# Order of the VectorE and GpSimd work in a merged LSTM and expert stage

## What is computed

```
# LSTM, 128 steps, one after the other (twice in this stage: layer 1 and layer 2)
z = x_t @ Wx + b + h @ Wh;  i, f, o, g = split(z)
c = sigmoid(f) * c + sigmoid(i) * tanh(g);  h = sigmoid(o) * tanh(c)

# expert block on the first LSTM's output, added to x
logits = a @ Wr + br;  the best two of 16 experts, with normalised softmax weights
h = layernorm(a @ W1[e] + b1[e]) * g1[e] + be1[e];  y = gelu(h) @ W2[e] + b2[e]
x = x + sum over the best two of weight * y
```

## Time and profile before

| | us |
|---|---|
| median of three runs | 4663.28 (4662.86 to 4663.63) |
| the profiled execution | 4662.41 |
| its span, first to last instruction | 4660.6 |
| the stage of the change | some 805, from about 1430 to 2235 |

### The profile page before, as it was taken

One profiled execution on the slowest core, in us unless ns is written; L12 is line 12 of the kernel. 1 busy time (PEld: TensorE's weight loads), 2 busy tenths in 40 slices (PEclk: granted clock), 3 DMA queues, 4 the chain that ended last, 5 costly groups with the idle time before them and its releaser, 6 DMA issues. The chain is left out here.

```text
span 4660.6 us, 118083 instructions
## 1 busy us (share of the span) xinstructions
PE 4309.6 (92%) x41087; PEld 3214.5 (69%) x41087; DVE 2494.8 (54%) x7506; ACT 1859.3 (40%) x4669; POOL 761.1 (16%) x3314
## 2 busy tenths in 40 slices
PE   6999999999998999998799999999997887889998
PEld 4556777777876888886355787787875555566666
DVE  5775664555554777776555444666666563421111
ACT  4433443333331444444233222666664452333333
POOL 1111220000001555554122000111111210000000
PEclk9999999999998999998699998999998997989999
DMA  1000000000000000000000000000000100000000
GB/s 53 0 0 25 0 0 25 0 0 0 0 0 10 1 2 1 1 1 1 33 1 0 3 0 0 3 3 3 3 3 2 52 0 1 0 1 0 0 0 18
DMA packets 3080, 28.73 MB, mean 6 GB/s; under 512 B 320, under 2 KB 832, under 8 KB 1216
## 3 DMA queue, kind: packets, MB, share of 16 engines
q1 hardware_dynamic: 2768, 24.81, 1.4%
HBM read 22.71 MB, written 2.10 MB: 5 GB/s over the span
## 5 line engine op out<-in xcount | busy, mean ns | idle before, releaser
L2231 DVE SCALAR_TENSOR_TENSOR experts_acc<-banks,experts_gate,experts_acc 128x128 f32<-128x128 f32 x512 | 144.2, 345 | 461.7 <-PE banks L2177 460.6
L2177 PEld LDWEIGHTS banks<-weights,experts_hidden 128*128 128x128 f32 x2560 | 303.3, 192 | 55.0 <-issue 49.7
L604 DVE TENSOR_REDUCE cells_row_max<-banks 128x4 f32<-128x512 f32 x384 | 238.5, 684 | 161.6 <-PE banks L397 161.6
L2177 PE MATMUL banks<-weights,experts_hidden 128*128 128x128 f32 x2560 | 305.2, 275 | 0.0
L761 PE MATMUL banks<-clock_fill 128*128 128x512 bf16 x932 | 284.8, 394 | 7.4 <-DVE wave_bias_parts L1612 7.4
L2450 ACT ACTIVATE experts_hidden<-banks,weights 128x512 f32<-128x512 f32 x256 | 175.8, 687 | 268.5 <-PE banks L2447 265.2
L1412 PEld LDWEIGHTS banks<-act_a,weights 128*128 128x128 f32 x2032 | 256.1, 196 | 25.6 <-DVE act_a L1670 18.0
L2447 PE MATMUL banks<-act_a,weights 128*128 (+1 forms) x512 | 262.3, 643 | 0.7 <-ACT experts_hidden L2450 0.3
L1412 PE MATMUL banks<-act_a,weights 128*128 (+1 forms) x2032 | 248.7, 281 | 10.8 <-DVE act_a L1670 10.7
L541 ACT ACTIVATE cells_probs<-banks 128x512 f32<-128x512 f32 x384 | 198.2, 603 | 95.0 <-PE banks L437 90.0
L604 DVE TENSOR_REDUCE attn_row_max<-banks 128x4 f32<-128x512 f32 x256 | 159.0, 684 | 134.8 <-PE banks L397 134.8
(11 more groups left out here) (522 smaller groups left out, 9904.5 us busy)
## 6 DMA issues: line engine op xcount, KB each, us to landing
weights<-in_p SPq DMA_DIRECT2D x1, 2894.5 KB, 17.2
weights<-in_p SPq DMA_DIRECT2D x1, 2894.0 KB, 9.2
weights<-in_p SPq DMA_DIRECT2D x2, 1364.0 KB, 7.1
x_res<-in_x SPq DMA_DIRECT2D x1, 2048.0 KB, 14.9
out_x<-x_res SPq DMA_DIRECT2D x1, 2048.0 KB, 6.3
weights<-in_p SPq DMA_DIRECT2D x1, 1836.0 KB, 10.9
weights<-in_p SPq DMA_DIRECT2D x1, 1835.5 KB, 6.9
weights<-in_p SPq DMA_DIRECT2D x1, 1344.5 KB, 9.8
```

Of the source, the lines that this page charges most:

```text
L604: dve.tensor_reduce(mt[:, 4 * g:4 * g + 4], bank, AX_X, ALU.max).then_inc(s["max_ready"], 1)
L2177: last = pe.matmul(ps[:, 2 + e % 2, t * P:(t + 1) * P], hs[lo:lo + n, (tile + f) % slots, t * P:(t + 1) * P], out_rhs(e, f, lo, n), start= ...
L2231: last = dve.scalar_tensor_tensor(out=acc[:, t, :], in0=ps[:, 2 + e % 2, t * P:(t + 1) * P], scalar=g[:, t, e:e + 1], in1=acc[:, t, :], op ...
```

## The change

Nothing is added to what is computed. On VectorE, `sums` and `guess` now stand ahead of `units`, and `add` comes last. The seventeen routing operations of a group are handed out one at a time: six places in the body (ahead of the cell, behind it, behind the state, between `sums` and `guess`, behind `units`, at the end). The semaphore `dist_ready` is gone: ScalarE's `distance` waits for the twelfth routing operation, which is the last of the second step, in the body's last place. On GpSimd, `tile_sum` stands ahead of `newton`, and the root has one operation less: the square is scaled by the root of 1/(2P), so that the sums are half the variance already, and the guess's constant is changed to fit (the third operation of a round is 1.5 - z in place of z + 1.5).

```diff
@@ GpSimd
             def newton(n, q):
                 pool.wait_ge(s["guess_ready"], n + 1)
                 past(pool, s["newton"], at)
-                pool.tensor_tensor(hv, v, newton_const[:, 0, :], ALU.mult).then_inc(s["newton"], 1)
                 for r in range(3):
                     pool.tensor_tensor(z, y, y, ALU.mult).then_inc(s["newton"], 1)
...
             def body(st, known):
+                it = item(st, SUM, known)
+                if it is not None and it[2] == 3:
+                    tile_sum(it[0], it[1], (st.c - SUM) // 4 % 2)
                 tile = tile_at(st, HSRC, known)
...
-                it = item(st, SUM, known)
-                if it is not None and it[2] == 3:
-                    tile_sum(it[0], it[1], (st.c - SUM) // 4 % 2)
@@ ScalarE
             def distance(group):
-                act.wait_ge(s["dist_ready"], group + 1)
+                act.wait_ge(s["route"], group * ROUTING + 12)
                 act.activation(dist[:, :], dist[:, :], ACT.Tanh, scale=0.5).then_inc(s["dist_tanh"], 1)
@@ VectorE
+            def route(st, known, at):
+                part_ = (st.c - ROUTE) % WAVE_PERIOD
+                group = group_at(st, part_, known) if part_ < 3 else None
+                if group is None or (part_, at) == (2, 5):
+                    return
+                done = group * ROUTING + (6 * part_ + at)
+                if part_ or at:
+                    dve.wait_ge(s["route"], done)
...
+                if part_ == 1:
+                    pick_best(at, work[:, :, :], m2, hot2, routed)
+                    if at == 5:
+                        past(dve, s["gates_ready"], group)
+                        routed(dve.tensor_tensor(dist[:, :], m1[:, :], m2[:, :], ALU.subtract))
...
             def body(st, known):
-                for part_, route in enumerate((route_first, route_second, route_gates)):
-                    group = group_at(st, part_, known)
-                    if group is not None:
-                        route(group)
+                route(st, known, 0)
                 cell(st, lo, hi)
+                route(st, known, 1)
                 tile = tile_at(st, LOGITS, known)
...
                 state(st, lo, hi)
+                route(st, known, 2)
+                it = item(st, HID, known)
+                if it is not None:
+                    sums(it[0], it[2])
+                    route(st, known, 3)
+                    guess(it[0], it[2])
+                else:
+                    route(st, known, 3)
+                it = item(st, UNIT, known)
+                if it is not None:
+                    units(it[0], it[2])
+                route(st, known, 4)
                 it = item(st, OUTPUT, known)
                 if it is not None:
                     add(st, *it)
-                it = item(st, UNIT, known)
-                if it is not None:
-                    units(it[0], it[2])
-                it = item(st, HID, known)
-                if it is not None:
-                    sums(it[0], it[2])
-                    guess(it[0], it[2])
+                route(st, known, 5)
```

More of the change, by code:

```diff
@@ L1226, in lstm_experts_lstm_stage @@
     RSRC, HSRC, GSRC = 4, 16, 20
-    NEWTON, ROUTING = 12, 15
+    NEWTON, ROUTING = 11, 16
     FOLD, FOLD_BIAS = (0, 2, 4, 5), 7
@@ L1255, in lstm_experts_lstm_stage @@
         sq = sb("square", [P, 2, 4, P + 1])
-        var, half_var, inv, part = (sb(n, [P, 2, 4]) for n in ("variance", "half_variance", "inverse", "part"))
+        half_var, inv, part = (sb(n, [P, 2, 4]) for n in ("half_variance", "inverse", "part"))
         shifted = sb("variance_shifted", [P, 2, 4], I32)
@@ L1546, in square @@
                 act.activation(sq[:, q % 2, :, 0:P], ps[:, HBANK + q % 2, :].rearrange("p (e j) -> p e j", e=4),
-                               ACT.Square, scale=float(P) ** -0.5).then_inc(s["square_ready"], 1)
+                               ACT.Square, scale=float(2 * P) ** -0.5).then_inc(s["square_ready"], 1)
             def gate_tanh(st, lo, hi):
@@ L1675, in logits @@
                                   ALU.add).then_inc(s["lg_ready"], 1)
-            def link(ins, group, n):
-                ins.then_inc(s["route"], 1)
-                dve.wait_ge(s["route"], group * ROUTING + n)
             over = lambda t: t[:, :].unsqueeze(2).broadcast_to([P, 4, NE])
             tie = const("tie16").unsqueeze(1).broadcast_to([P, 4, NE])
[L1685 to L1691, removed]
@@ L1693, in route_first @@
-            def route_first(group):
-                dve.wait_ge(s["lg_ready"], group * 4 + 4)
-                values = lg[:, tok(group * 4, 4), :]
[L1696 to L1713, removed]
+            def pick_best(at, values, top, hot, routed):
+                if at == 0:
+                    routed(dve.tensor_reduce(top[:, :], values, AX_X, ALU.max))
+                if at == 1:
+                    routed(dve.tensor_tensor(hot[:, :, :], values, over(top), ALU.is_equal))
+                if at == 2:
+                    routed(dve.tensor_tensor(hot[:, :, :], hot[:, :, :], tie, ALU.mult))
+                if at == 3:
+                    routed(dve.tensor_reduce(best[:, :], hot[:, :, :], AX_X, ALU.max))
+                if at == 4:
+                    routed(dve.tensor_tensor(hot[:, :, :], hot[:, :, :], over(best), ALU.is_equal))
@@ new lines, in route @@
+            def route(st, known, at):
[6 more added lines that the diff above has]
+                    dve.wait_ge(s["route"], done)
+                routed = lambda ins: ins.then_inc(s["route"], 1)
+                values = lg[:, tok(group * 4, 4), :]
+                if part_ == 0:
+                    if at == 0:
+                        dve.wait_ge(s["lg_ready"], group * 4 + 4)
+                    pick_best(at, values, m1, hot1, routed)
+                    if at == 5:
+                        routed(dve.scalar_tensor_tensor(out=work[:, :, :], in0=hot1[:, :, :], scalar=-1.0e30,
+                                                        in1=values, op0=ALU.mult, op1=ALU.add))
+                if part_ == 1:
+                    pick_best(at, work[:, :, :], m2, hot2, routed)
+                    if at == 5:
+                        past(dve, s["gates_ready"], group)
+                        routed(dve.tensor_tensor(dist[:, :], m1[:, :], m2[:, :], ALU.subtract))
+                if part_ == 2:
+                    if at == 0:
+                        routed(dve.tensor_tensor(work[:, :, :], hot1[:, :, :], hot2[:, :, :], ALU.subtract))
+                    if at == 1:
+                        routed(dve.tensor_tensor(hot1[:, :, :], hot1[:, :, :], hot2[:, :, :], ALU.add))
+                    if at == 2:
+                        dve.wait_ge(s["dist_tanh"], group + 1)
+                        routed(dve.tensor_tensor(work[:, :, :], work[:, :, :], over(dist), ALU.mult))
+                    if at == 3:
+                        routed(dve.tensor_tensor(hot1[:, :, :], hot1[:, :, :], work[:, :, :], ALU.add))
+                    if at == 4:
+                        dve.tensor_scalar(gates[:, tok(group * 4, 4), :], hot1[:, :, :], 0.5, None,
+                                          ALU.mult).then_inc(s["gates_ready"], 1)
@@ L1725, in guess @@
                 past(dve, s["unit_ready"], n - 1)
[L1726 to L1727 removed]
+                dve.tensor_scalar(inv[:, q % 2, :].bitcast(I32), shifted[:, q % 2, :], -1.0,
+                                  float(0x5F3759DF - 0x400000), ALU.mult, ALU.add).then_inc(s["guess_ready"], 1)
             def units(n, q):
```

18 lines of the change are left out of this document (9 added, 9 removed).

## The result

The changed kernel takes 4690.42 us, the median of four runs (4687.94 to 4694.72), against 4663.45 for the kernel before (four runs, 4662.86 to 4668.53): a ratio of 1.0056, with a 95% interval of 1.0039 to 1.0074. It is slower by some 27 us, outside the range of 4647 to 4681. The profiled execution took 4688.42 us, its span is 4686.4, its mean granted clock 0.954 (before: 4662.41, 4660.6 and 0.959).

What follows compares the result with a forecast made beforehand. TensorE was taken to bound the middle, a closed GpSimd-VectorE ring the head and tail. Terms -12 + 9 + 2 + 4 = +3 us on 4662.4, median 0.9 above: forecast 4666, own range 4655 to 4676, with rivals 4647 to 4681.

Steps and rivals of the forecast that it cites:

- Part 1: Head and tail: with sums and guess ahead of the scaling, a step takes 4.1 us instead of 5.2, VectorE-bound.
- The ring: Head and tail steps: GpSimd's root (3.43 us) and VectorE's scaling, sums and guess (1.8 us) form a closed 5.2 us.
- the ends: Head (steps 21 to 31) and tail (129 to 149) of the stage: forecast -12 us, bounds -18 to -5.
- the hold: Every fourth step: partial sums ahead of the root delay it to 3.6 us behind the next state in the ends.
- Part 2: Partial sums ahead of the root: fours in the ends take 18.8 us against 20.9; plain middle fours cost nothing.
- Part 3: Middle, six routing groups: late distance tanh makes TensorE stand 2.5 us; 2.7 in place of 1.2 each, +9 us.
- Part 4: Middle, four loop back edges: gap ends 0.4 us earlier, late adds hold others; 2.1 in place of 1.6, +2 us.
- Part 5: Clock falling around each routing group's TensorE stand: 0.7 us taken per group, +4 us in all.
- (b): Rival, every fourth middle step: root's hold outgrows its 0.18 us slack at VectorE's scaling; +15 us, 4681, chance 0.17.
- (a): Rival, routing groups: ScalarE's wait for the twelfth operation costs nothing, groups gain 1.0 us each; 4647, chance 0.24.
- (c): Rival, head and tail: nothing gained, another wait takes the ring's place; +12 us, 4678, chance 0.11.

Runs made afterwards that it cites:

- e1: The kernel before with only VectorE's order changed (sums, guess, scaling, adds): 4632.92 us, ratio 0.9926.
- e5: The changed kernel with GpSimd's partial sums put back behind the root: 4646.55 us, ratio 0.9952 to the kernel before.
- e6: The changed kernel with the gated additions ahead of the scaling, partial sums still ahead of the root: 4650.89 us, ratio 0.9960 to the kernel before.
- e7: The changed kernel with useless matmuls, two ahead of each total and eight ahead of the third routing step's gate turn: 4671.55 us, ratio 1.0007 to the kernel before.
- e8: The changed kernel with partial sums behind the root and ScalarE's distance tanh behind the cell's tanh: 4622.97 us, ratio 0.9905 to the kernel before.
- e2: The kernel before with only GpSimd's partial sums moved ahead of the root: 4671.48 us, ratio 1.0007.
- e4: The changed kernel with ScalarE's distance tanh moved behind the cell's tanh of the same step: 4682.03 us, ratio 1.0026 to the kernel before.
- e3: The kernel before with routing one by one, distance tanh waiting for the twelfth operation, and one root operation less: 4678.07 us, ratio 1.0019.

## Why the prediction was wrong

**Part 1, sums and guess ahead of the scaling: right, and too small.** The ring opens, L1332 is gone, and with the order alone the ends win 7.7 + 16.2 = 24 us (e1), more than the -18 that I gave as its bound; the whole change without the hold (e5) wins 18.8 there, about that bound. Only the shortest open steps take 3.94 us against my 4.1; in e1 the others take 4.2 to 4.9. I had also left the middle out of this part, where it won 10.6 us.

**Part 2, partial sums ahead of the root: this is the step that failed.** The hold's size was right (additions over at 3.59, forecast 3.70; scaling of a held tail step from 3.13 us, forecast 3.6). The sentence "TensorE covers the hold in plain middle fours" asked only whether VectorE is done by its next cell. It did not ask who else waits for the last thing in VectorE's queue. The total does, for its bank, and it is due before the cell. In the tail this makes two long steps of each four (6.77 and 5.87 where I had 6.3 and 4.15), and the 12 us of the ends did not come. With the partial sums back behind the root (e5) or the additions ahead of the scaling (e6) they do come: 18.8 and 17.8 us. In the middle the plain fours, but for one (42 to 45), did keep their 21.5 us wherever the clock held, stand of 0.4 us and all; what I missed there is what such a stand can do to the clock.

**Part 3, routing one by one: the mechanism was right, its size too large.** The tanh starts 3.0 us behind the state where I had 3.7, as the sums began right behind the state and a routing operation on VectorE cost next to nothing where it began before the one ahead of it ended (scaling over at 1767.03, additions from 1767.08), not 0.25 us; TensorE stands 1.6 us, not 2.5. Without the clock a group costs 0.8 us more than before (e7), where I had 1.5. With it, the six groups cost 18.7 us, where I had 9.

**Part 4, back edge: wrong in sign, small.** The cell behind the edge starts 4.36 us behind the state in place of 6.36:

```profile
1817.43 0.25 DVE L1654 SCALAR_TENSOR_TENSOR wave_fc<-wave_gates_tanh,wave_c_twice 128x64 f32<-128x64 f32 x1 [1.59 <-ACT wave_gates_tanh L1551]
```

The row names ScalarE, but that tanh was over 0.8 us earlier, so some "issue" is left in the 1.59 us; before it was 3.10. My "ends some 0.4 earlier" let the gap begin with the last operation and kept its length. The other half was right: the late additions hold the total of the step after next by 1.4 to 1.5 us (forecast: its store, by 1.2 to 1.4). Together the four takes 22.8 us where the clock holds, against 23.1 to 23.2 before, and 21.5 to 21.6 in e5, which has no hold.

**Part 5, clock: the term most mis-sized.** I had +4 us. Half clock in the middle went from 6.8 to 54.6 us, and a microsecond at half rate loses at most half of its matmul work: at most 23.9 us for the 47.8 more, where the matmuls grew by 18.8. e7 tests it: filling the stands brings half clock to 10.2 us and the middle to 541.4, 8.6 us above before and near the +9 and +2 of Parts 3 and 4, which had no clock in them. I had priced 0.7 us of loss per group; a fall costs a plain four 1.6 to 1.7 us (23.10 against 21.44), it came in every group, TensorE was at half clock twice as long in three of the six groups, and I had given none to any other step.

The sum so fails twice: ends +1.3 in place of -12, and the middle +26.7 in place of +15 (9, 2 and 4). Of the rivals, (b) had the place, the partial sums' hold in every fourth middle step, but not the way: it put the cost on scaling and cell, and those were in time. (a) is out: the tanh does cost. (c) came true in the changed kernel, near its price of 12 us: the ends gained nothing, as another wait took the ring's place. It is the total's, which (c) did not name; the hidden layer queues behind it, and so the square is late. The ends can gain where that wait is short (e1, e5, e6, e8).

**The port rule.** The Trainium skill ("SBUF — State Buffer", section "SBUF: two separate sides"), by which a VectorE operation with two SBUF inputs and a GpSimd operation that reads SBUF hold one another up, had spoken against the change. The trace agrees: in step 141 a cell operation that takes 0.19 us elsewhere begins beside the partial sum and ends with it, after 0.62 us.

```profile
2193.73 0.72 POOL L1348 TENSOR_TENSOR wave_sum_of_two<-wave_acc 128x256 f32<-128x256 f32 x1 [1.96 <-DVE wave_acc L1766]
...
2193.88 0.62 DVE L1659 SCALAR_TENSOR_TENSOR wave_c_twice<-wave_fc,wave_ic 128x32 f32<-128x32 f32 x1
```

It costs some 0.4 us in one step of four in the tail and decides nothing: in e8, the fastest kernel, the same kind of operation takes 0.65 to 0.79 us beside a partial sum in twelve steps of the middle.

**What stays open.** Which stand brings a fall. Before, TensorE stands 1.3 to 1.55 us at the store in all six first routing steps and 0.7 to 0.9 us behind each back edge; the clock falls behind two of the edges and at none of the stores. After, the 1.6 us ahead of the gate turn bring a fall six times out of six, the 1.4 to 1.5 us at the total in three of five (94, 110, 126), and the 0.4 us there in a few. Nor does the length alone tell: in e2 TensorE stands 1.6 to 2.1 us at the store in the six first routing steps, and the clock falls behind one of them. No run varied one stand's length alone. Nor did I try the total behind the outputs on TensorE. Half clock differs between executions of one kernel too (e4's mean granted clock is 0.951 to 0.958), and each count here is of one.

## What to carry to other kernels

When an operation is moved to the end of an in-order queue, list everything that waits for it on every engine, banks to be freed included, and take the earliest time at which any of them wants it; the slack of the next operation on its own engine is not the slack of the move. On an engine that is the bound, price a new stand at its length and once more for the clock, and look for the other stands nearby: in the middle, by one trace each, taking one of two away brought 3.4 or 19.6 us, taking both 43.6. A change of several reorderings is worth splitting, as here one part alone won 0.7% and another one turned the sum into a loss.

## What the runs showed of the hardware

A stand of 1.6 us on TensorE ahead of the gate turn, between steps in which it works all but throughout, came with half clock in all six places of the changed kernel, in all six of e5 and in five of six in e6. The stands of 1.6 to 2.1 us ahead of the outputs in e2 did so in one place of six. In e4 the stands at the total are 0.4 to 0.9 us in 18 steps and 1.4 to 1.5 in five, and half clock came in 15 of these 23. In e8, where only one gap of over 0.15 us is left ahead of a total and none ahead of a gate turn in the groups, it never came in the middle. Filling the idle with matmuls of no use shortened the middle by 18.1 us, although 96 matmuls (25.9 us busy) were added to the busiest engine.

The 3.10 us of "issue" on VectorE at the back edge are no fixed price. VectorE is idle there for 2.9 to 3.2 us in all three kernels whose step ends with sums and guess (before, e2, e3), and for 1.5 to 1.8 us in all seven in which these stand ahead of the scaling; e1 changes nothing but that order. Why the order does it is not shown.
